# The first unit's round moved into PE's loop of turns, with two branches on the counter, in a windowed attention kernel (Trainium2, one core)

## The reference

```
x = x + zca(gn(x))        # whitening in 16 groups of 4 channels: cov -> inverse square root -> 4x4 product
x = x + attention(gn(x))  # batch norm, then windows of 7 x 7 strided positions:
    tok  = windows of 49 tokens, 64 channels                  # 16 * 8 * 8 = 1024 windows
    q, k = (tok @ qk_w.T).reshape(-1, 49, 2, 16, 16)          # the reshape folds four windows into one group of 16 heads of 16
    attn = softmax(q @ k.T * 16 ** -0.5)                      # 49 x 49 for each head and group
    o    = attn @ relu(tok @ v_w.T).reshape(-1, 49, 16, 16)
```

## Time and profile before

| | before |
|---|---|
| median of 3 runs | 457.76 us (457.18 to 458.96) |
| the profiled execution, its own time | 457.5 us |
| its span, first to last instruction | 455.8 us |
| PE busy | 416.3 us, 91% |
| PEld (weight loads) busy | 336.6 us, 74% |
| DVE busy | 359.3 us, 79% |
| ACT busy | 288.4 us, 63% |
| POOL busy | 186.8 us, 41% |

### The profile page before, as it was taken

One profiled execution on the slowest core, in us unless ns is written; L12 is line 12 of the kernel. 1 busy time (PEld: TensorE's weight loads), 2 busy tenths in 40 slices (PEclk: granted clock), 3 DMA queues, 4 the chain that ended last, 5 costly groups with the idle time before them and its releaser, 6 DMA issues. The chain is left out here.

```text
span 455.8 us, 38218 instructions
## 1 busy us (share of the span) xinstructions
PE 416.3 (91%) x17218; PEld 336.6 (74%) x17218; DVE 359.3 (79%) x1157; ACT 288.4 (63%) x489; POOL 186.8 (41%) x156
## 2 busy tenths in 40 slices
PE   7799528886879999999999999999999999999993
PEld 6688424334658888888888888888888888888883
DVE  2587688774568888888888888888888888888884
ACT  3388603777546676676776666766767667677651
POOL 6200000200325554455554455544555544555332
PEclk9999859999999999999999999999999999999998
DMA  8997000011114342414252343424142523424233
GB/s 289 416 401 321 1 1 0 1 72 38 66 49 124 107 150 79 142 71 151 89 150 89 123 124 107 150 79 142 71 152 87 150 89 124 126 104 151 79 106 74
DMA packets 32714, 55.20 MB, mean 121 GB/s; under 512 B 6304, under 2 KB 21152, under 8 KB 31776
## 3 DMA queue, kind: packets, MB, share of 16 engines
q1 hardware_dynamic: 32672, 54.71, 35.4%
HBM read 16.16 MB, written 12.85 MB: 64 GB/s over the span
## 5 line engine op out<-in xcount | busy, mean ns | idle before, releaser
L379 POOL TENSOR_TENSOR X<-X,otok 128x392 f32<-128x392 f32 x63 | 107.8, 1711 | 160.4 <-DVE otok L830 160.4
L790 DVE TENSOR_REDUCE rmax<-ps 113x16 bf16<-113x784 f32 x128 | 124.1, 970 | 45.2 <-PE ps L971 45.1
L1009 PE MATMUL ps<-diag,qk_all 64*49 64x98 f32 x4096 | 128.5, 244 | 0.2 <-ACT prob_all L445 0.2
L1009 PEld LDWEIGHTS ps<-diag,qk_all 64*49 64x49 f32 x4096 | 105.8, 120 | 22.9 <-issue 22.5
L1023 PE MATMUL ps<-mdiag,sel 64*49 64x98 bf16 x2048 | 111.4, 204 | 0.0
L373 POOL TENSOR_SCALAR xs<-X,affined 128x392 f32<-128x392 f32 x64 | 69.9, 1092 | 98.9 <-DVE affined L776 70.1
L445 ACT ACTIVATE prob_all<-ps 113x784 f32<-113x784 f32 x128 | 105.5, 824 | 6.0 <-PE ps L1023 4.4
L460 ACT ACTIVATE vst<-ps 49x256 f32<-49x256 f32 x193 | 73.0, 378 | 54.6 <-PE ps L955 52.2
L452 ACT ACTIVATE qk_all<-ps 128x784 f32<-128x784 f32 x64 | 52.7, 824 | 51.5 <-PE ps L935 51.3
L1023 PEld LDWEIGHTS ps<-mdiag,sel 64*49 64x49 bf16 x2048 | 63.0, 99 | 0.8
L1054 PE MATMUL ps<-prob_all,vst 113*32 113x49 f32 x4096 | 59.0, 208 | 3.3 <-issue 3.3
(11 more groups left out here) (168 smaller groups left out, 374.3 us busy)
## 6 DMA issues: line engine op xcount, KB each, us to landing
diag<-qk_all SPq DMA_DIRECT2D x256, 98.0 KB
out<-X SPq DMA_DIRECT2D x30, 392.0 KB
X<-x_in SPq DMA_DIRECT2D x7, 1024.0 KB, 14.0
X<-x_in SPq DMA_DIRECT2D x7, 544.0 KB, 15.1
diag<-x_in SPq DMA_DIRECT2D x8, 392.0 KB, 12.4
X<-x_in SPq DMA_DIRECT2D x4, 256.0 KB, 3.7
out<-X SPq DMA_DIRECT2D x2, 294.0 KB
X<-x_in SPq DMA_DIRECT2D x2, 192.0 KB, 4.7
```

What stands on the lines that cost most here:

```text
L379: g.tensor_tensor(rows_of(u), rows_of(u), otok[u % 2][:].rearrange("p k a s -> p k s a"), ALU.add).then_inc(S["x_ready"], 1)
L790: v.tensor_reduce(rmax[u % 3][0:ROW, :, 8 * k:8 * k + 8], ps[0:ROW, B_S:B_S + 2, 0:8 * POS].rearrange("p h (v q) -> p h v q", q=POS), AX.X ...
L1009: ins = mm(ps[64 * e:64 * e + POS, B_ST + hh, col:col + 2 * POS], qk[u % 3][r, g, k, 2 + x_, :], diag[u % 3][r, e::2, g, k, x_, :], start= ...
```

## The change

PE's loop gets one turn more (22), begins with `rest(4)` in place of `rest(1)`, and the whole of its first two rounds is left out in turn 0 by a branch on the counter. What is left of turn 0 is `project_qk(2)`, the round of unit 0 in the form of `rest(3)`, and `project_qk(3)`. The third round, with the `project_qk` ahead of it, is left out in the last turn. The straight code ahead of the loop is gone. The order of the rounds is the same, with these differences:

- Unit 0's round now also does `sum_weights` and `weigh_values` for a unit -1, on `prob[2]` and `vst[2]`. So that these hold numbers, ACT fills `prob[2]` with zeros from `diag[0]` ahead of the mix steps; all waits on `zeros_ready` go from 3 to 4. The counts of `den_ps` and `pv_ps` are one higher, and who waits for them adds one.
- `project_qk(65)` is gone. Its waits on `v_ready` and `v_dve` now stand ahead of the last `weigh_values`.
- Semaphore `v_dve` starts with a credit of 1, `prob1` gets one increment by ACT behind the mix steps, and tokens of unit 3 are signalled on `xs_ready` in place of `xs_head`; the wait on `xs_head` for unit 2 stands ahead of the loop.

```
-        CREDIT = {"rden_ready": 4, "o_ready": 4}
+        CREDIT = {"rden_ready": 4, "o_ready": 4, "v_dve": 1}
...
-                                ALU.mult, ALU.add).then_inc(S["xs_head" if u < 4 else "xs_ready"], 1)
+                                ALU.mult, ALU.add).then_inc(S["xs_head" if u < 3 else "xs_ready"], 1)
...
             for b in range(1, 3):
                 a.activation(diag[b][:]..., diag[0][:]..., ACT.Copy).then_inc(S["zeros_ready"], 1)
+            a.activation(prob[2].rearrange("p k h g x j s -> p (k h g x j s)"),
+                         diag[0][:].rearrange("p j g k a s -> p (j g k a s)")[:, 0:2 * 8 * 2 * POS], ACT.Copy).then_inc(S["zeros_ready"], 1)
...
             def weights(u, k):
-                after(act, "pv_ps", u - 2)
+                after(act, "pv_ps", u - 1)
...
+            act.sem_inc(S["prob1"], 1)
             for i in range(0, UNITS + 1):
...
             def invert(u):
-                dve.wait_ge(S["den_ps"], u + 1)
+                dve.wait_ge(S["den_ps"], u + 2)
...
             def project_qk(u):
                 if u == 1:
                     pe.wait_ge(S["qk_head"], 1)
-                if u < 4:
+                if u < 2:
                     pe.wait_ge(S["xs_head"], u + 1)
...
             def weigh_values(u):
                 if u >= UNITS - 2:
                     pe.wait_ge(S["o_ready"], u + CREDIT["o_ready"])
+                if u == UNITS - 1:
+                    pe.wait_ge(S["v_ready"], 1)
+                    pe.wait_ge(S["v_dve"], 1)
...
-            project_qk(2)
-            rest(0)
-            project_qk(3)
-            with pe.Fori(0, 21) as turn:
-                rest(1)
-                project_qk(4)
-                rest(2)
-                project_qk(5)
-                with pe.If(turn < 20):
+            pe.wait_ge(S["xs_head"], 3)
+            with pe.Fori(0, 22) as turn:
+                with pe.If(turn > 0):
+                    rest(4)
+                    project_qk(7)
+                    rest(5)
+                with pe.If(turn < 21):
+                    project_qk(5)
                     rest(3)
                     project_qk(6)
             for i in range(63, UNITS + 1):
                 rest(i)
```

More of the change, by code:

```diff
@@ L312, in store @@
                                  ).then_inc(S["stored"], 16)
-            sp.wait_ge(S["zeros_ready"], 3)
+            sp.wait_ge(S["zeros_ready"], 4)
             for u in range(UNITS):
@@ L465, in _ @@
             act.wait_ge(S["dd_ready"], 1)
-            act.wait_ge(S["zeros_ready"], 3)
+            act.wait_ge(S["zeros_ready"], 4)
             for n in range(MIX):
@@ L498, in _ @@
             steps = [0]
-            give(dve, "rden_ready", "o_ready")
+            give(dve, "rden_ready", "o_ready", "v_dve")
             def chain(ins):
@@ L796, in rest_of_values @@
                 dve.wait_ge(S["v_half"], u)
-                after(dve, "pv_ps", u - 2)
+                after(dve, "pv_ps", u - 1)
                 out, in_ = values_of(u, 1, 1)
@@ L825, in divide @@
             def divide(u):
-                dve.wait_ge(S["pv_ps"], u + 1)
+                dve.wait_ge(S["pv_ps"], u + 2)
                 dve.wait_ge(S["rb_ready"], 4 * (u + 1))
@@ L832, in divide @@
                                 ).then_inc(S["o_ready"], 1)
-            dve.wait_ge(S["zeros_ready"], 3)
+            dve.wait_ge(S["zeros_ready"], 4)
             for n in range(13, MIX):
@@ L1093, in _ @@
                     pe.wait_ge(S["const_dma"], 48)
-                    pe.wait_ge(S["zeros_ready"], 3)
+                    pe.wait_ge(S["zeros_ready"], 4)
                     project_qk(0)
```

## The result

| | before | after |
|---|---|---|
| median | 457.47 us of 4 runs (456.74 to 458.96) | 470.58 us of 4 runs (469.12 to 474.1) |
| ratio | | 1.0286, 95% interval 1.0251 to 1.0322 |
| the profiled execution | 457.5 us, span 455.8 | 469.94 us, span 468.2 |

The account below looks back on a forecast made before the run. PE's instruction stream was taken to bound the kernel: 457.5 us plus 3.4 (start), 2.2 (steady turns) and 0.7 (tail) made 463.8, and with 0.26 for the median of runs 464.0 us; range 459.9 to 467.3.

Parts of the forecast that it names:

- Start, the jump: Turn 0's branch over two rounds: the target is not yet fetched, so PE waits 3.7 us, from 106.8 to 110.5.
- the edges 595 and 720: Code block edges 595 and 720 pairs behind the loop's head: PE waits there in turn 0, until 114.2 and 117.9 us.
- Start, what is known in turn 1: Turn 1: only blocks jumped over are fetched, other code is known; second full turn at 138.8, start +3.4 us.
- Three blocks that turn 0 jumped over are new: Turn 1: three skipped code blocks must be fetched, arriving at 122.9, 126.6 and 130.3 us.
- From the third edge (345) on, 411 pairs at 0.0207 are 8.5 us: Rest of turn 1, from 345 pairs behind the loop's head: runs at full pace without fetches, ending at 138.8 us.
- The pace of fetching: Code PE meets for the first time: 3.7 us from one block's arrival to the next.
- Exposed compare: Steady turns: uncovered compare between turn_max and project_qk costs 0.09 us in 20 turns, 1.8; with the loop head's 0.4, 2.2.
- Unit 0's 96 extra pairs: Turn 0: new sums and weighted values, 2.0 us of PE, lie under the waits for code and add nothing.
- The clock rival: PE's nearly 5 us without matmuls at the jump lowers the clock: +1 to +2 us, some 465.5; chance 0.15.
- The loop no longer stays in the store: Rival: jumping throws code blocks out, so turns fetch again, 1 us or more in each of 20: 480 and more; chance 0.04.
- Tail: Behind the loop: a moved code edge makes PE wait inside the last L1041, +0.4 to +1.1 us, taken as 0.7.
- more packets than 20: Sign that the forecast is wrong: PE's code queue carrying over 20 packets; 17 were expected in place of 18.

Follow-up runs that it names:

- e9: e2 with 209 instructions more of warm-up far ahead of the loop, so the jump starts earlier in its code block: 484.17 us, ratio to before 1.0578.
- e2: The changed kernel with its first turn jumping over one round in place of two: 475.8 us, ratio to before 1.0433.
- e10: The changed kernel with both warm-up loops written out, 64 instructions more ahead of the loop: 465.04 us, ratio to before 1.0175.
- e7: The kernel before with one real compare between turn_max and project_qk, project_qk(65) left out, no jump forward: 459.73 us, ratio 1.0048.
- e3: The changed kernel with project_qk ahead of the second branch and project_qk(65) done again: 469.61 us, ratio to before 1.0249.
- e1: The changed kernel's order of work in 21 whole turns without any branch but the loop's own: 465.46 us, ratio to before 1.0162.
- e8: e1 with one project_qk moved ahead of the loop and the others to the ends of their rounds: 460.56 us, ratio to before 1.0073.
- e11: The changed kernel run once more, unaltered, for a second profile: 470.98 us.
- e6: The kernel before with both warm-up loops written out, 64 instructions more ahead of the loop: 460.19 us, ratio 1.0046.

## Why the prediction was wrong

- **Start, the jump**: right in size, 3.77 us against 3.7. That turn 0 then ended at 119.35 against 119.2 was luck. The two waits that I had put at the edges 595 and 720 do not show; the 260 pairs ran without a break, for 8.4 us in place of 5.4, at a granted clock of 0.50 up to 116 us.
- **Start, what is known in turn 1**: this step failed. "Back at the head, 95 pairs, known code" held; "Three blocks that turn 0 jumped over are new" held; "From the third edge (345) on, 411 pairs at 0.0207 are 8.5 us" did not. I had taken the store to keep every block once read. Blocks behind a hole did not stay, so the blocks of the 411 pairs were fetched again: they took 13.2 us (131.49 to 144.70) in place of 8.5. These 4.7 us are the larger part of a miss of 6.1 in the profiled executions. Six code packets in turn 1, where three blocks were new, show the fetches; e9 against e2 shows it with the instructions of the loop unchanged; e10 shows which block stays.
- **The pace of fetching**: forecast 3.7 us a block, in after's turn 1 4.0. With the late end of turn 0 it brought the third edge to 131.5 in place of 130.3, 1.2 us. So the second full turn came at 144.7 in place of 138.8, 5.9 us late.
- **Exposed compare**: right in mechanism, a little too high. Forecast 2.2 us for both compares, measured 0.08 us a turn, 1.5 to 1.6 (after); the place was shown alone by e7 (0.07 a turn) and by e3. The reason given, no cover between `turn_max` and `project_qk`, holds for the taken branch as well, at 0.3 us (e1, e8). An estimate from the figures of the Trainium skill ("Advanced Engine Details and Errata", Control Flow Timing) was 3.2; the runs disagree.
- **Unit 0's 96 extra pairs**: I put them at nothing, under the waits for code. In after no run separates them. Without the jump the start is 0.7 (e8) to 1.4 us (e1) longer than before, little beyond the scatter, so a cost of them is likely but not shown.
- **The clock rival** (0.15) came true in its mechanism and not in its price. The granted clock was 0.70 from 107 to 113 us and 0.77 from 113 to 120, and the slow clock took the place of the waits for code that the forecast had put there, not time on top of them.
- **"The loop no longer stays in the store"** (0.04) was the right family: jumping did throw blocks out. I priced it only as a loss in every turn. It happens once: after turn 1, which fetches the blocks in order, the turns run at their length again (15.71 us).
- **Tail**: right, 0.8 against 0.7, at the place named. The 1.2 us DMA wait was not foreseen, nor the last store's 0.9 us the other way.
- Among the signs I had named were "more packets than 20". With 21, they told against my picture of the store, though 20 in e11 would not have.

## What to carry to other kernels

Count a forward jump over cold code as one fetch (3.3 to 5.0 us here) plus a new fetch, in the next turn, of everything behind the skipped blocks, whether it was read or not; only in e2, where the one block skipped was already being fetched, was there no second fetch. Compare that with the straight code it saves. Put loop ends and Ifs behind instructions that run long on the engine: the same compare was free behind `project_qk` and cost 0.07 us in front of it, a taken branch 0.3 us. When timing an added branch, see in the trace that the branch exists.

## What the runs showed of the hardware

- With a hole between them, blocks read a turn earlier were fetched again (turn 1: 25.57 us and six packets against 16.25 us and one, e9 and e2), although 7 blocks have room, as all steady turns show. One unbroken sequence of blocks is the rule that fits all runs here; how the store does it inside is not shown. The Trainium skill ("Runtime: NRT & Kernel Launch", Instruction fetch mechanics) calls the store a FIFO with purely sequential prefetch and gives 128 KiB for PE, which is 8 blocks of 16 KiB. The 7 blocks that stay agree with that size, and the "only 2 cache lines" of the same section does not. Of a taken branch it says that a target outside the window forces a fetch before execution goes on, as the jumps here show (3.77 us in after). That known blocks are fetched again behind a hole it does not say, and a plain FIFO of 8 blocks would still have held blocks 4 to 6 in after.
- A jump into missing code took 3.3 to 3.8 us in after, e9, e10 and e11, and 4.7 and 5.0 us in e3 and e2. In these two the code queue carried two packets during the jump, in the others one: the next block was being fetched as well.
- Where the loop's head lies in its block went with large changes of the time, by the ratios: 5.1 us less for after (64 instructions, e10), 6.6 us more for the one-round jump (209 instructions, e9), 2.1 us more for before (the same 64, e6).
